# Two mask rows under queries and keys, second attention's splits made by GpSimd from a copy, and a new order, in a fused decoder layer

## The reference

```python
x = _layernorm(x + attn(x))              # latent attention: 16 heads of 8, causal, 256 keys
x = _layernorm(x + xattn(x, ctx_1024))   # keys and values from 512 context rows, then x's 256
x = _layernorm(x + ffn(x))               # 128 -> 64, 64 small MLPs of 16, -> 128
# in both attentions
dots = einsum('bhid,bhjd->bhij', q, k) * 8 ** -0.5
attn = softmax(where(later key than query, -inf, dots))
out = einsum('bhij,bhjd->bhid', attn, v)
```

## Time and profile before

| what | value |
|---|---|
| three runs | 254.71, 261.5, 261.26 us |
| profiled execution | 251.84 us, span 249.8 us |
| busy TensorE / VectorE / ScalarE / GpSimd | 227.6 / 192.3 / 181.2 / 109.7 us |
| mean granted TensorE clock | 0.993 |

### The profile page before, as it was taken

One profiled execution on the slowest core, in us unless ns is written; L12 is line 12 of the kernel. 1 busy time (PEld: TensorE's weight loads), 2 busy tenths in 40 slices (PEclk: granted clock), 3 DMA queues, 4 the chain that ended last, 5 costly groups with the idle time before them and its releaser, 6 DMA issues.

```text
span 249.8 us, 7711 instructions
## 1 busy us (share of the span) xinstructions
PE 227.6 (91%) x2963; PEld 140.4 (56%) x2963; DVE 192.3 (77%) x424; ACT 181.2 (73%) x391; POOL 109.7 (44%) x290
## 2 busy tenths in 40 slices
PE   8998897879997989899999999999999999999971
PEld 5676675557775746455464444564454544556651
DVE  1197787966979796899999999989999976344533
ACT  3256877887988787689957966878778988894420
POOL 8924379584665166633318413315332216241321
PEclk9999999999999997999999999999999999999999
DMA  3938920479999895870004700000000000000000
GB/s 93 372 112 238 179 31 1 130 202 167 273 174 271 182 196 127 191 125 5 3 2 130 125 5 4 5 2 3 1 4 4 1 4 4 0 24 0 25 21 21
DMA packets 20536, 21.57 MB, mean 86 GB/s; under 512 B 1244, under 2 KB 18196, under 8 KB 20372
## 3 DMA queue, kind: packets, MB, share of 16 engines
q1 hardware_dynamic: 20356, 20.96, 37.1%
q10 hardware_dynamic: 144, 0.13, 0.2%
HBM read 11.85 MB, written 9.18 MB: 84 GB/s over the span
## 4 chain that ended last, share of the span: by engine, by line
PE 38%; DVE 26%; POOL 14%; ACT 8%; issue 6%; DMA 4%; SPq 1%; POOLq 0%; ACTq 0%; DVEq 0%
DVE pm L1036 13%; PE psum L1289 10%; DVE pm L1038 6%; PE psum L1232 6%; ACT probs L934 5%; PE psum L1133 3%; PE psum L1212 3%; DMA qk<-scr_qk 3%; DVE left L1053 2%; PE psum L1251 2%; DMA scr_qk<-spl 2%; PE psum L1199 2%; POOL rstd L895 1%; ACT spl L953 1%; POOL km L697 1%
## 5 line engine op out<-in xcount | busy, mean ns | idle before, releaser
L934 ACT ACTIVATE probs<-psum 128x512 f32<-128x512 f32 (+1 forms) x256 | 118.2, 554 | 18.3 <-PE psum L1232 13.9
L1036 DVE TENSOR_REDUCE pm<-psum 128x1 f32<-128x512 f32 x128 | 79.5, 681 | 2.7 <-PE psum L1212 2.5
L1038 DVE TENSOR_REDUCE pm<-psum 128x3 f32<-128x384 f32 x128 | 63.1, 549 | 6.2 <-PE psum L1199 5.9
L1289 PE MATMUL psum<-probs,v 128*18 128x256 f32 (+3 forms) x1024 | 61.5, 356 | 0.9 <-ACT probs L934 0.5
L1289 PEld LDWEIGHTS psum<-probs,v 128*18 128x18 f32 (+1 forms) x1024 | 26.2, 94 | 18.7 <-ACT probs L934 5.2
L1212 PE MATMUL psum<-km,qk 51*128 51x512 bf16 x128 | 35.0, 386 | 0.6 <-ACT probs L934 0.3
L1232 PE MATMUL psum<-qk,km 51*128 51x256 bf16 x256 | 33.5, 276 | 0.3
L1232 PE MATMUL psum<-qk 51*128 51x256 bf16 (+1 forms) x256 | 31.9, 246 | 1.9 <-DVE y L1080 0.9
L866 POOL TENSOR_SCALAR_AFFINE_SELECT probs<-probs 128x512 f32<-128x512 f32 x32 | 19.8, 639 | 30.4 <-ACT probs L934 30.4
L1199 PE MATMUL psum<-neg,unit_b 64*128 64x128 bf16 (+1 forms) x256 | 30.9, 242 | 0.0
L849 POOL CAST max_s<-maxima 128x8 bf16<-128x8 f32 x32 | 6.1, 191 | 53.5 <-DVE maxima L1043 53.4
(11 more groups left out here) (127 smaller groups left out, 335.1 us busy)
## 6 DMA issues: line engine op xcount, KB each, us to landing
qk<-scr_qk SPq DMA_DIRECT2D x14, 384.0 KB, 6.6
km<-scr_m SPq DMA_DIRECT2D x8, 384.0 KB, 8.2
scr_qk<-spl SPq DMA_DIRECT2D x7, 384.0 KB, 3.0
scr_qk<-spl SPq DMA_DIRECT2D x21, 128.0 KB, 3.1
scr_m<-spl SPq DMA_DIRECT2D x4, 384.0 KB, 3.8
ctxT_sb<-ctxT SPq DMA_DIRECT2D x1, 1024.0 KB, 6.8
scr_m<-spl SPq DMA_DIRECT2D x4, 256.0 KB, 3.8
wb_sb<-wb SPq DMA_DIRECT2D x1, 642.0 KB, 4.8
```

Of the source, the lines that this page charges most:

```text
L934: nc.scalar.activation(probs[:, ring % PRING, r, 0:cols], bank_of(s)[:, 0:cols], ACT.Exp, scale=SCALE).then_inc(exp_done, 1)
L1036: nc.vector.tensor_reduce(pm[:, place, 1 + 4 * qt:2 + 4 * qt], m, axis=AX.X, op=ALU.max).then_inc(reduced, 1)
L1038: nc.vector.tensor_reduce(pm[:, place, 2:5], own_blocks(m), axis=AX.X, op=ALU.max).then_inc(reduced, 1)
L1289: last = nc.tensor.matmul(o, v[:, at:end], weights, start=(k == 0 and not second), stop=(k == len(key_tiles(t)) - 1 and second == 1), skip ...
```

## The change

1. The two halves of a tile hold two more rows (`OWN_ROWS`, 53) for units 1 to 7. Under the queries they hold minus 3e38 for the first 64 queries of the first block (and for the first 64 of the second block), under the keys ones for the later 64 keys of each block: their product masks the quarter of each block in which all keys are later. So each of the two mask products of these units has 2x64 columns. Unit 0 keeps the mask of before.
2. The constants are no longer memset but copied on GpSimd from two pattern tiles (`under_queries`, `under_keys`) that it builds first, with two memsets and ten affine selects. Unit 4's keys get a copy too.
3. Splits of units 4 to 7 and of the context: ScalarE copies the bank, as float32, into `left`, and GpSimd rounds the high part, subtracts it, and goes on as before. VectorE has no part in these eight splits.
4. The planner's tables change (`low` on GpSimd from 1950 to 3800, fewer columns for masked tiles, other priorities), and with them the whole order.

```diff
+OWN_ROWS = ROWS + 2
-LATE = [(("qk", 0), 0), (("qk", 1), 0), (("qk", 2), 0), (("v1", 0), 2), (("qk", 3), 4), (("v1", 1), 0), (("m", 0), 9),
-        (("vm", 0), 10), (("m", 1), 10), (("vm", 1), 14), (("m", 2), 14), (("vm", 2), 19), (("m", 3), 15),
-        (("vm", 3), 26)]
+LATE = [(("qk", 0), 0), (("qk", 1), 0), (("qk", 2), 0), (("v1", 0), 5), (("qk", 3), 5), (("v1", 1), 0), (("m", 0), 2),
+        (("vm", 0), 10), (("m", 1), 15), (("vm", 1), 15), (("m", 2), 18), (("vm", 2), 23), (("m", 3), 11),
+        (("vm", 3), 24)]
...
-POOL_COST = {"hilo": 1100, "causal": 600, "rstd": 1320, "after": 870, "pow": 1100, "low": 1950}
+POOL_COST = {"hilo": 1100, "causal": 600, "rstd": 1320, "after": 870, "pow": 1100, "low": 3800}
...
+def patterned(u):
+
+    return u > 0
...
         def zeros_under(engine, queries):
-            return engine.memset(queries.bitcast(F32), 0.0)
+
+            return engine.tensor_copy(queries.bitcast(F32), under_queries[:, :].bitcast(F32).unsqueeze(1).to_broadcast([P, PAIRS, T // 2]))
+
+        def rows_under(engine, keys):
+
+            return engine.tensor_copy(keys.bitcast(F32), under_keys[:, :].bitcast(F32).unsqueeze(1).to_broadcast([P, PAIRS, T // 2]))
...
+            nc.gpsimd.memset(under_queries[:, :].bitcast(F32), 0.0).then_inc(under_ready, 1)
+            nc.gpsimd.memset(under_keys[:, :].bitcast(F32), ONES).then_inc(under_ready, 1)
+            pool.wait_ge(under_ready, 2)
+            for r in range(2):
+                for tile, fill, first, places in ((under_queries, NEG, ROWS, (0,)), (under_queries, NEG, ROWS + 1, (P,)),
+                                                  (under_keys, 0.0, ROWS, (0, P)), (under_keys, 0.0, ROWS + 1, (HALF,))):
+                    for at in places:
+                        cols = half(tile, r, HALF)[:, at:at + HALF]
+                        nc.gpsimd.affine_select(out=cols, in_=cols, compare_op=ALU.is_ge, fill=fill, base=first - 1, pattern=[[0, HALF]],
+                                                channel_multiplier=-1).then_inc(under_ready, 1)
+            pool.wait_ge(under_ready, 12)
             for u in range(1, B):
-                ones_under(nc.gpsimd, qk[:, u, :, 1, :]).then_inc(qk_ones, 1)
+                rows_under(nc.gpsimd, qk[:, u, :, 1, :]).then_inc(qk_ones, 1)
                 zeros_under(nc.gpsimd, qk[:, u, :, 0, :]).then_inc(qk_ones, 1)
...
                 elif s in split_no and not low_on_dve(s):
                     i = split_no[s]
-                    pool.wait_ge(split_left, i + 1)
+                    pool.wait_ge(split_left[i], 1)
+                    whole, high = left[:, i % SPL, :], parts_of(s)[0]
...
+                    nc.gpsimd.tensor_copy(high, whole).then_inc(split_high[i], 1)
+                    pool.wait_ge(split_high[i], 1)
+                    nc.gpsimd.tensor_sub(whole, whole, high).then_inc(split_high[i], 1)
+                    pool.wait_ge(split_high[i], 2)
                     rest, mid, low = low_parts(nc.gpsimd, s)
...
+                        if s[1] == B:
+                            rows_under(nc.gpsimd, qk[:, 0, :, 1, :]).then_inc(first_keys, 1)
                         zeros_under(nc.gpsimd, qk[:, s[1] % B, :, 0, :]).then_inc(blanked, 1)
...
-                    nc.scalar.activation(parts_of(s)[0], m, ACT.Copy).then_inc(split_high, 1)
+                    if low_on_dve(s):
+                        nc.scalar.activation(parts_of(s)[0], m, ACT.Copy).then_inc(split_high[i], 1)
+                    else:
+                        nc.scalar.activation(left[:, i % SPL, :], bank_of(s), ACT.Copy).then_inc(split_left[i], 1)
...
-                    if (what == "S") == (n == 0):
+                    if patterned(u):
+                        block, part = o[:, :, HALF * n:HALF * (n + 1)], rows[:, 0:HALF] if what == "S" else rows[:, HALF:]
+                    elif (what == "S") == (n == 0):
                         block, part = o, rows
```

More of the change, by code:

```diff
@@ L1208, in score @@
                 p, r = 2 * g + j // 2, j % 2
-                queries, keys = (half(qk[:, u % B, p, a, :], r, ROWS) for a in range(2))
+                rows = OWN_ROWS if src == "own" and patterned(u) else ROWS
+                queries, keys = (half(qk[:, u % B, p, a, :], r, rows) for a in range(2))
                 m = bank_of(s)
@@ L1223, in score_pair @@
                 q0 = P if n == 1 else 0
+                rows = ROWS if n is None or not patterned(u) else OWN_ROWS
                 m = bank_of(s)
```

64 lines of the change are left out of this document (36 added, 28 removed).

## The result

The changed kernel takes 260.52 us (median of five runs, 258.95 to 265.66). Beside it the kernel before took 261.26 us (252.85 to 261.67). The kernel before has runs with a granted clock near 0.99 (span 250 us) and runs near 0.94 (span 259 us), and the ratio of the two kernels is formed from the faster runs of each only. It is **1.0253, with a 95% interval of 1.0198 to 1.0308: slower**, where 0.987 was forecast. That 260.5 lies in the forecast range is luck of the base: 261.26 was the median of three runs, two of which took as long as runs at the low clock do (their own clocks are not on record). Over the 76 further runs that the kernel before had beside the experiments its median is 255.9 us.

What follows compares the result with a forecast made beforehand. VectorE's reductions were taken to bound the second attention, TensorE close behind and nearest in the first. +3.3 − 2.6 − 3.9 = −3.2 us on 251.84 us, a ratio of 0.987, gave 257.9 us on the median, range 248 to 264 us.

Steps and rivals of the forecast that it cites:

- The new order: Whole kernel: unit 2's normalization moving ahead of the second attention counted 1.8 us; the earlier first context write cost nothing.
- The end: T, pv and MLP stages after the last reduction: taken as 0, with 1 us either way.
- Start: GpSimd's constant copies take turns with VectorE's three splits, delaying unit 1's split and first score: +3.3 us, bounds 0 to 10.2.
- Masks: TensorE, first attention: 128 fewer mask columns per tile, paired halves, −2.6 us; second attention taken as 0.
- Splits and the moved normalization: VectorE, second attention: three subtractions fewer (2.1 us) and unit 2's normalization moved ahead (1.8 us): −3.9 us.
- Rival (b): GpSimd's longer qk splits, with maxima queued behind, give back the middle's gains: +0.8 us, median 262.1 us; chance 0.13.
- Rival (c): GpSimd's copies take 2.3 us each and the start slips 10.2 us: +6.6 us, median 268.1 us; chance 0.10.
- (a): TensorE is the true bound and masks gain unpaired: −11.2 us, median 249.6 us; chance 0.27.
- The prediction's own test: First context reduction to last maxima: about 131 us if right, 134 or more if GpSimd or order gave gains back.

Runs made afterwards that it cites:

- e3: The kernel before with the changed kernel's planner tables and exact order; memsets, old masks and old splits stay: 260.14 us, ratio 1.0287.
- e7: The kernel before, in its own order and with its splits, given only the new masks and pattern copies: 260.46 us, ratio 1.0120.
- e9: The kernel before, own order and splits, with new masks and pattern copies, units 2 and 3's constants written later: 254.98 us, ratio 1.0019.
- e5: The kernel before with idle TensorE products ahead of unit 0's split and the first S and T of five steps: 260.29 us, ratio 1.0101.
- e10: The changed kernel with masks added as before; its order, splits and constants stay: 259.91 us, ratio 1.0252 to the kernel before.
- e11: The changed kernel with the second attention's splits made as before; its order and masks stay: 260.99 us, ratio 1.0256 to the kernel before.
- e15: The changed kernel with paced constants, vm 2 earlier, apply wo 0 later and unit 7's split as before: 255.20 us, ratio 1.0032.
- e8: The kernel before, in its exact order, with all the change's instructions (masks, copies, GpSimd's splits): 268.71 us, ratio 1.0538.
- e12: The changed kernel with stage vm 2 allowed at step 22 instead of 23: 260.66 us, ratio 1.0210 to the kernel before.
- e2: The changed kernel planned with the old tables; masks, copies and splits stay as changed: 278.54 us, ratio 1.1003 to the kernel before.
- e14: The changed kernel with paced constants, vm 2 earlier and ScalarE's apply wo 0 behind step 21's exponentials: 257.07 us, ratio 1.0113.
- e1: The changed kernel with eight idle TensorE products just ahead of the wait for unit 0's split: 260.69 us, ratio 1.0209.
- e6: The changed kernel with idle TensorE products ahead of unit 0's split and the first S and T of five steps: 258.43 us, ratio 1.0147.

## Why the prediction was wrong

- **The new order: the step that failed.** The prediction counted what the order moves (a normalization, a put) and priced the order itself at nothing; "The end" was given 0. e3 shows the order alone at +2.5 us at equal clock, with a ratio of 1.0287. Its profile has the 22nd to 24th step at 20.01 us against 17.24, with 33 more products of TensorE in it (247 against 214), and "The end" at 41.26 us against 39.74: 1.5 us where 0 was taken. What was missing is what stands *between* two score tiles and behind each wait at the places where projections, a split and a layer norm meet; the order could have been read for that.
- **The clock was no term.** TensorE's clock of 1.00 from 17.60 to 74.50 us was taken as given, and the forecast was scaled to the median by a ratio. e7 and e9 differ only in when the constants are written: their clocks are 0.941 and 0.966, which is 4.2 us by the line. Why the clock falls when it does stays open. The three runs of before, 254.71 against 261.5 us, were a sign that this kernel's time moves of itself.
- **Start, +3.3 us.** Right in kind: copies of 1.04 and 1.23 us (taken 1.15), ending at 17.77 us (17.6), subtractions of 1.14 and 1.25 us in turns with them. The size was half: +1.6 us. A turn took 1.17 us where 1.5 was played (three of them stand ahead of the end of unit 1's split), and the second cast took 0.54 us, not 0.9. But unit 1's first score was 5.5 us late, not 3.3. In the profile of before, TensorE waited 0.76 us for the data ahead of it; after, it had no wait there and worked at the clock of 0.50. All of this is read from an execution that starts late. In one that starts early the memsets hold the first cast for 4.43 us (e3), and e5, the kernel before with idle products, shows the same: a cost of memsets that the profile of the kernel before doesn't show and that copies take away.
- **Masks, −2.6 us.** Not seen in the time of the new order (e10 is 0.6 us below the changed kernel), 1.2 ± 1.0 us there at equal clock, and 1.1 ± 0.6 us in the old order, together with the pacing (e9). TensorE busy 50.66 of 56.90 us was read as a bound; less than half of the price is seen.
- **Splits and the moved normalization, −3.9 us.** VectorE's busy time in its window fell by 2.5 us and its idle time rose by 6.6. e11 gives the subtractions back to VectorE for 0.5 us of median, within the scatter. Less work for VectorE shortened nothing, since TensorE's scores came later.
- **Rival (b)** was right in kind: the maxima do queue behind GpSimd's split. e15 prices it at 1.2 us of that stretch for unit 7 (1.4 us of the whole at equal clock, ± 0.8); e8 at 5.7 us in all where the order leaves no room. It was given 0.13. Rival (c) fell with the copies' 1.04 us, and (a) with e10.
- The prediction's own test, the window at 134 us or more with exponentials behind late maxima, pointed the right way: 138.63 us.

## What to carry to other kernels

An order is a change of its own: run it alone, with the old instructions, before pricing the work that it was made for. Before you take work from a busy engine, see whether the engine that takes it has somebody waiting behind it at that place; look for the two or three places where a long job stands ahead of a short one that others wait for. And with one core's clock moving between runs, compare spans at equal clock, from many runs of the kernel before, since the median of three misled by 5 us here. The same holds for a stretch of a profile: read its clock, and how much each engine had to do in it, before you call its length a wait.

## What the runs showed of the hardware

- GpSimd's copy of 128x1024 float32 takes 1.04 us and, beside VectorE's two-tile subtractions, 1.23 us; the memset of that size takes 0.95 us.
- A VectorE cast of 128x512 that takes 0.43 us alone was held for 4.43 us (e3) and 4.26 us (e5) while GpSimd wrote memsets one after the other, and ended 0.3 us behind the last. Beside GpSimd's copies it took 0.43 to 1.23 us (e10, e12, after).
- One kernel's span moved with the mean granted clock by 1.7 us per 0.01, from 249.2 us at 0.993 to 259.9 us at 0.936, and runs at both ends occurred in one series.
- The clock fell to 0.50 after TensorE had been nearly idle (busy for 0.01 us of the 3 before 15 us in e3, for 0.02 in e5) and also straight after work: in e9's profile TensorE was busy for 0.99 of the 1 us before it. The changed kernel held 1.00 from 14 to 16 us, where TensorE was busy for 1.14 of 2 us, and lost it four microseconds later.
- In all nine profiles whose first subtraction starts at 8.9 to 9.7 us (e2 to e5, e9, e10, e12 to e14) the clock fell to 0.50 between 14 and 18 us. Of the eight that start it at 11.94 us, it fell at 20 us in the five with copies in a row and at most eight idle products (after, e1, e7, e8, e11), and it stayed at 1.00 until 24 us in before, in e6 with more idle products and in e15 with paced copies. What brings the fall about stays open.
